# High parts of the FFN operands on GpSimd, softplus read from PSUM, x1 in two slots, new step tables, in a Mamba block with a ternary FFN

## The chip, the core and the metric

The kernel runs on one core of a Trainium2 chip. Engine names are those of the profile: PE is TensorE's matrix multiplication and PEld its weight load, DVE is VectorE, ACT is ScalarE, POOL is GpSimd, SP is SyncE. PSUM is the memory that PE writes, SBUF the working memory. The metric is the device time of one execution in microseconds (us), the median of the runs.

## The reference

Sixteen sequences of 512 tokens and 256 channels pass a selective scan layer and a feed-forward network, each followed by a residual sum and a layer norm:

```python
xr = x @ in_w.T; xx, res = split(xr)            # 512 + 512 channels
xx = silu(causal_conv4(xx) + conv_b)
delta, B, C = split(xx @ xproj_w.T)             # 16, 16, 16
delta = softplus(delta @ dt_w.T + dt_b)
h[l] = exp(delta*A) * h[l-1] + delta*B*xx       # 16 states a channel
y = (sum over states of h*C + xx*D) * silu(res)
x1 = layernorm(x + y @ out_w.T)
h = silu(x1@w1.T*w1_s) * (x1@w2.T*w2_s)         # 1024 wide
h = gelu(h@h1.T*h1_s); h = gelu(h@h2.T*h2_s)
out = layernorm(x1 + h@w3.T*w3_s)
```

The weights of the FFN hold -1, 0 and 1 times a factor. Everything is float32.

## The kernel before

A sequence is a "row". Four rows are in work at a time: `rows(i, par)` gives the one whose scan runs in iteration i (`scan` = i), the one whose inputs to the scan are made (`front` = i+1), the one whose scan is over and that is gated, projected, normed and sent into the FFN (`tail` = i-1), and the one whose FFN ends (`end` = i-2). An iteration has 64 steps, one for each of 16 states times 4 blocks of 128 channels. Every engine runs the same loop over the steps, `iteration(i, par)`, and tables of step numbers say in which step it issues which piece of the other rows' work. So the order on each engine is written out by hand. Engines meet through semaphores alone, and a step has no fixed length. FFN steps from 64 on are those of the next iteration less 64 (`ffn_step(end, s + TILES)`).

**The scan.** For a pair of steps ACT makes `dA` (L607, exp, in a ring of 8 tiles, 4 or more steps ahead) and `dB` (L616, 7 steps ahead), PE transposes dB into `scan_ps` in PSUM (L367, `b_pair`, issued one pair ahead; there are two buffers of a pair), DVE scans the pair in an even step (L782) and multiplies it by C into `hC` in the odd one (L792, two buffers), and POOL issues a DMA that adds hC to `y2` (L968, `y_pair`). hC of pair p waits until the addition of pair p-2 has landed.

**The front.** x is transposed and projected, and the convolution is made by ACT and DVE (L630, L806). PE multiplies for delta in four blocks c in the steps `F_DT` (L423) into the one bank `misc_ps`. DVE adds the bias one step later and frees the bank (L818, `dt_ready`). Softplus is max(z,0) + log(1+exp(-|z|)) with a correction of the rounding in 1+exp: Abs and Exp on ACT (L650, L652, into `du`), 1+e on DVE (L829, into `sp_w[c]`, `F_PLUS`), the lost part on DVE (L831), max less the lost part on DVE (L837, `F_MAX`), Ln on ACT (L656, step 51), the sum (L843) and times u (L848) on DVE in the steps 54 and 55.

**The FFN.** Weights are exact in float32r. Each operand is split in two float32r parts, high and low, and PE multiplies both. `half_tile` (32 of them a row, table `HALF_AT`) makes 8 matmuls of 128x512 on half of the inputs of one tile; L479 is the line of `products`, which all FFN matmuls go through. A tile of 128 outputs then goes ACT Gelu (L688, into the ring `x32` of 4 tiles), ACT Copy to the high part (L697, `hi_tiles`; in the first layer L710), POOL subtraction to the low part (L990, `low_tile`). The Gelu of tile i waits for the low part of tile i-4, and PE waits for low parts at the start of a layer. The first layer's `l1_tile` (8 of them, steps 22 to 29) is 8 matmuls, a Tanh (L705) and two DVE operations (L899, L906) of a tile. `w3_tile` (`E_W3`) makes the last product. DVE scales it (L914), adds x1 (L921) and makes the statistics (L862) and the norm (L873).

```python
dst = hb_hi if i < HC else ha_hi
nc.scalar.activation(dst[:, i % HC, :], x32[:, i % X32, :], ACT.Copy).then_inc(ffn_hi, 1)
...
pool.wait_ge(ffn_hi, f * FFN_TILES + (i + 1))
nc.gpsimd.tensor_tensor(lo[:, i % HC, :], x32[:, i % X32, :], hi[:, i % HC, :].bitcast(F32),
                        ALU.subtract).then_inc(ffn_lo, 1)
```

In the steps that hold a Gelu (`NO_EXP`) ACT makes no dA; these are made in steps before, since Exp and Gelu need different tables (ACT_TABLE_LOAD).

Of the kernel before, what the change touches and what calls it, by code (L numbers as in the profile page):

```python
# [1070 lines left out]
```

## Time and profile before

| | |
|---|---|
| median of 3 runs | 3148.1 us (3145.47 to 3153.55) |
| the profiled execution, its time and its span | 3155.7 us, 3153.9 us |
| PE, DVE, ACT, POOL busy | 2583.1, 2621.1, 2343.3, 1071.0 us |
| first scan begins, last scan ends | 83.2 us, 3001.3 us |
| the 15 rows after the first | 284.9 to 3001.3 us, 181.1 us each |
| mean granted TensorE clock | 0.897 |

The span is the time from the first to the last instruction on the core. A busy time is the union of an engine's instructions. A stretch of the trace is named here by the steps of the scan: "steps 40 to 56" is the time from the start of DVE's scan of step 40 to that of step 56. Other engines are some steps ahead or behind.

### The profile page before, as it was taken

What the parts mean: (1) busy time and instruction counts of PE and PEld (TensorE: products, weight loads), DVE (VectorE), ACT (ScalarE), POOL (GpSimd) and SP (SyncE); (2) the same over time, 40 slices, a digit from 0 to 9 for tenths busy, and PEclk for the clock granted to TensorE, in tenths of its full rate; (3) what the DMA queues carried; (4) which work ended last, traced back from release to release, by engine and by line L of the source; (5) the groups of instructions that cost most, each with busy time, mean ns of one, the idle gap of its engine ahead of it and who ended that gap; (6) DMA issues with size and microseconds to landing.
All of it is one profiled execution on the core that took longest, in us unless ns stands there. A gap on an engine that the chain in (4) does not pass through costs nothing.

```text
span 3153.9 us, 41504 instructions
## 1 busy us (share of the span) xinstructions
PE 2583.1 (82%) x12290; PEld 1944.8 (62%) x12290; DVE 2621.1 (83%) x2625; ACT 2343.3 (74%) x3653; POOL 1071.0 (34%) x1028
## 2 busy tenths in 40 slices
PE   4355788888888888988888898888888889898888
PEld 1223566676666666676666766666676756666666
DVE  3678998989898897989889898988989898998830
ACT  2776687877969787796968779697877969687822
POOL 0112333333433433343343334234333423423432
PEclk8566899999989999999989999899999989899999
DMA  1996787787878778787887878787787878778933
GB/s 52 290 321 140 167 193 180 185 197 184 194 179 193 190 181 186 183 194 183 190 188 179 194 181 194 179 196 189 178 190 181 200 186 196 189 180 191 229 111 110
DMA packets 230192, 585.49 MB, mean 186 GB/s; under 512 B 26016, under 2 KB 26400, under 8 KB 229808
## 3 DMA queue, kind: packets, MB, share of 16 engines
q0 software_dynamic: 73728, 268.47, 46.2%
q1 hardware_dynamic: 119344, 246.86, 22.4%
q10 hardware_dynamic: 36864, 67.13, 7.9%
q8 instruction: 115, 1.88, 0.2%
q14 instruction: 141, 1.16, 0.1%
HBM read 281.93 MB, written 31.98 MB: 100 GB/s over the span
## 4 chain that ended last, share of the span: by engine, by line
PE 32%; DVE 29%; ACT 17%; issue 14%; DMA 4%; ACTq 1%; DVEq 1%; SPq 1%; POOL 1%; POOLq 0%
PE ffn_ps L479 17%; DVE scan_ps L782 11%; DVE hC L792 5%; PE scan_ps L367 5%; ACT dB L616 4%; ACT dA L607 3%; DVE y L806 3%; PE misc_ps L372 3%; DMA x<-ffn_w 3%; PE misc_ps L423 2%; DVE gate L899 2%; PE misc_ps L460 2%; PE misc_ps L408 2%; ACT L607 2%; PE misc_ps L367 2%
## 5 line engine op out<-in xcount | busy, mean ns | idle before, releaser
L782 DVE TENSOR_TENSOR_SCAN scan_ps<-dA,scan_ps 128x1024 f32<-128x1024 f32 x512 | 1170.8, 2287 | 57.0 <-PE scan_ps L367 33.2
L968 POOL DMA_DIRECT2D y<-hC x512 | 446.1, 871 | 1811.2 <-DVE hC L792 1735.1
L367 PE MATMUL scan_ps<-ident,dB 128*128 128x128 f32 x4096 | 613.4, 300 | 375.7 <-DVE hC L792 292.3
L367 PEld LDWEIGHTS scan_ps<-ident,dB 128*128 128x128 f32 x4096 | 519.9, 154 | 521.2 <-DVE hC L792 305.5
L616 ACT ACTIVATE dB<-duT,bT 128x512 f32<-128x512 f32 x1024 | 726.4, 711 | 154.5 <-PE scan_ps L367 153.2
L607 ACT ACTIVATE dA<-delta,a_neg 128x512 f32<-128x512 f32 (+1 forms) x1024 | 710.1, 712 | 41.1 <-DVE hC L792 38.0
L479 PE MATMUL ffn_ps<-hb_hi,ring 128*128 128x512 f32 x1536 | 660.1, 430 | 18.4 <-DVE gate L899 8.7
L792 DVE TENSOR_TENSOR hC<-scan_ps,c_rows_sb 128x1024 f32<-128x1024 f32 x512 | 623.6, 1218 | 49.8 <-DMA y<-hC 41.5
L479 PE MATMUL ffn_ps<-hb_lo,ring 128*128 128x512 f32 x1536 | 620.7, 404 | 0.0
L479 PE MATMUL ffn_ps<-ha_hi,ring 128*128 128x512 f32 x1024 | 443.5, 433 | 2.4 <-POOL ha_lo L990 2.4
L479 PE MATMUL ffn_ps<-ha_lo,ring 128*128 128x512 f32 x1024 | 407.7, 398 | 0.0
L990 POOL TENSOR_TENSOR ha_lo<-x,ha_hi 128x512 fp32r<-128x512 f32 x256 | 356.0, 1492 | 89.8 <-ACT ha_hi L697 52.8
L479 PEld LDWEIGHTS ffn_ps<-hb_hi,ring 128*128 128x128 f32 x1536 | 304.6, 198 | 108.4 <-DVE gate L899 29.6
L479 PEld LDWEIGHTS ffn_ps<-hb_lo,ring 128*128 128x128 f32 x1536 | 303.4, 198 | 64.2 <-issue 7.4
L372 PE MATMUL misc_ps<-out_st,inw 128*128 128x512 f32 x512 | 282.3, 679 | 27.5 <-DVE y L806 25.5
L479 PEld LDWEIGHTS ffn_ps<-ha_hi,ring 128*128 128x128 f32 x1024 | 197.8, 193 | 94.9 <-issue 55.5
L479 PEld LDWEIGHTS ffn_ps<-ha_lo,ring 128*128 128x128 f32 x1024 | 197.8, 193 | 48.9 <-issue 12.8
L688 ACT ACTIVATE x<-ffn_ps,fs 128x512 f32<-128x512 f32 x256 | 166.9, 685 | 72.1 <-PE ffn_ps L479 69.7
L990 POOL TENSOR_TENSOR hb_lo<-x,hb_hi 128x512 fp32r<-128x512 f32 x128 | 194.3, 1570 | 33.2 <-ACT hb_hi L697 33.0
L705 ACT ACTIVATE gate<-ffn_ps,s_half 128x512 f32<-128x512 f32 x128 | 87.7, 685 | 116.0 <-PE ffn_ps L479 116.0
L372 PEld LDWEIGHTS misc_ps<-out_st,inw 128*128 128x128 f32 x512 | 100.6, 216 | 115.9 <-issue 74.3
L806 DVE SCALAR_TENSOR_TENSOR y<-misc_ps,conv_half,y 128x511 f32<-128x511 f32 (+2 forms) x192 | 143.3, 747 | 31.0 <-ACT y L630 26.5
(90 smaller groups left out, 2941.9 us busy)
## 6 DMA issues: line engine op xcount, KB each, us to landing
y<-hC POOLq DMA_DIRECT2D x512, 512.0 KB, 5.8
ring<-split_weights SPq DMA_DIRECT2D x704, 256.0 KB, 4.3
c_rows_sb<-c_rows ACTq DMA_DIRECT2D x256, 256.0 KB, 4.0
xt<-x_tok SPq DMA_DIRECT2D x32, 512.0 KB, 6.1
x<-ffn_w SPq DMA_DIRECT2D x22, 512.0 KB, 9.7
split_weights<-ha_hi SPq DMA_DIRECT2D x22, 512.0 KB, 5.2
split_weights<-ha_lo SPq DMA_DIRECT2D x22, 512.0 KB, 7.0
out_tok<-out_st SPq DMA_DIRECT2D x16, 512.0 KB, 2.9
```

Of the source, the lines that this page charges most:

```text
L367: mm = nc.tensor.transpose(dst[:, j * P:(j + 1) * P], src(j), ident[:])
L372: mm = nc.tensor.matmul(misc_ps[:], inw[:, k, col * P:(col + 1) * P], xT[:, k, :], start=(k == 0), stop=(k == KD - 1))
L479: mm = nc.tensor.matmul(dst, w, a, start=(first and n == 0), stop=(last and n == len(steps) - 1))
L607: nc.scalar.activation(dA[:, s % DA_RING, s % 2:], delta2[:, par, c, s % 2:], ACT.Exp, scale=a_neg[:, c, n:n + 1]).then_inc(dA_ready, 1)
L616: nc.scalar.activation(dB[:, n % 2, t, :], duT[:, t, :], ACT.Copy, scale=bT2[:, par, t, n:n + 1]).then_inc(dB_ready, 1)
L688: nc.scalar.activation(x32[:, i % X32, :], ffn_ps[(2 * HC + i) % 3][:], ACT.Gelu, scale=fs[:, 2 + i // HC, i % HC:i % HC + 1]).then_inc(ge ...
L705: nc.scalar.activation(gate[:, o % 2, :], ffn_ps[2 * o % 3][:], ACT.Tanh, scale=s1_half[:, o:o + 1]).then_inc(l1_tanh, 1)
L782: nc.vector.tensor_tensor_scan(b, dA[:, a:a + 2, :].rearrange("p a l -> p (a l)"), b, 0.0, ALU.mult, ALU.add).then_inc(scan_done, 1)
L792: nc.vector.tensor_tensor(hC[:, p % 2], scan_ps[:, h:h + 2, :], c_rows[:, n % 2].unsqueeze(1).to_broadcast([P, 2, SEQ]), ALU.mult).then_in ...
L806: nc.vector.scalar_tensor_tensor(out=y2[:, par, c, back:], in0=misc_ps[:, 0:SEQ - back], scalar=conv_half[:, c, tap:tap + 1], in1=y2[:, pa ...
L968: pool.dma_start(y2[:, par, c:c + 2, :], hC[:, p % 2], accum_op=ALU.add).then_inc(y_added[p % 2], 16)
L990: nc.gpsimd.tensor_tensor(lo[:, i % HC, :], x32[:, i % X32, :], hi[:, i % HC, :].bitcast(F32), ALU.subtract).then_inc(ffn_lo, 1)
```

## The change

1. `hi_tiles` and `low_tile` become one `split_tile` on POOL: a `tensor_copy` makes the high part, and the subtraction follows. ACT loses 24 Copy operations of 128x512 a row, and POOL gets 24 copies.
2. Delta before softplus is not stored. ACT reads the PSUM bank twice, with the bias: Abs into `du` and Relu into `delta2`, then Exp. DVE loses the addition L818 and the maximum L837. The lost part and max(z,0) are joined in another way: POOL adds exp(-|z|) to Relu(z) (`base_step`, `F_BASE`), DVE makes (w-1) less that sum (`F_LOST`), and the last operation on DVE is Ln less this (the lines L831 and L843 of before, with other operands).
3. `x1` has two slots, so that the next row may write it before the row that ends has read it.
4. The step tables are new, two PE waits are added that guard the banks of PSUM, and EXP_COUNT puts the dA tiles that a Gelu step leaves out into the latest steps before it that hold fewer than three.
5. The SBUF space for the descriptors of POOL's DMAs is set to 8192 bytes a partition.

```diff
-HALF_AT = [33, 34, 35, 36, 37, 38, 40, 41, 42, 43, 44, 45, 47, 48, 49, 50,
-           54, 55, 56, 57, 58, 59, 61, 62, 63, 64, 65, 66, 68, 69, 70, 71]
-GELU_AT = {39: (0, 1), 40: (2,), 46: (3, 4), 47: (5,), 51: (6, 7), 52: (),
-           60: (8, 9), 61: (10,), 67: (11, 12), 68: (13,), 72: (14, 15), 73: ()}
-HI_AT = {40: (0,), 41: (1,), 42: (2,), 47: (3,), 48: (4,), 49: (5,), 52: (6, 7),
-         61: (8,), 62: (9,), 63: (10,), 68: (11,), 69: (12,), 70: (13,), 73: (14, 15)}
-T_RES, T_GATE = (0, 3, 6, 8), (2, 5, 7, 10)
-T_OUT, T_ADD, T_STATS, T_NORM, T_X1T = (12, 13, 14, 15), (15, 17), (16, 18), 19, (20, 21)
-E_W3, E_SCALE, E_ADD, E_STATS, E_NORM = (11, 12, 13, 14), (15, 16), (16, 17), (19, 20), 22
-F_DT, F_EXP, F_PLUS, F_MAX, F_LN = (41, 42, 43, 44), (43, 44, 45, 48), (44, 45, 46, 49), (45, 46, 47, 50), 51
-F_DELTA, F_DELTA_U, F_Y, F_DU = (54, 54, 55, 55), (54, 54, 55, 55), (57, 58, 59, 60), (56, 57, 58, 59)
+T_RES, T_GATE = (0, 3, 5, 8), (3, 4, 7, 11)      # the tables of after, in fewer lines
+T_OUT, T_ADD, T_STATS, T_NORM = (12, 13, 15, 17), (15, 18), (16, 18), 19
+E_W3, E_SCALE, E_ADD, E_STATS, E_NORM = (10, 11, 13, 14), (12, 16), (14, 19), (15, 21), 22
+L1_AT = (22, 23, 24, 25, 26, 27, 28, 29)
+L1_SPLIT_AT = (22, 24, 25, 27, 28, 29, 30, 31)
+HALF_AT = (31, 32, 34, 35, 36, 38, 40, 41, 42, 43, 45, 46, 47, 48, 49, 50, 51, 52, 53, 54, 55, 57, 59, 60, 62,
+           63, 64, 65, 66, 68, 69, 71)
+GELU_AT = (38, 38, 39, 46, 46, 47, 50, 51, 56, 57, 58, 66, 66, 67, 72, 72)
+SPLIT_AT = (37, 40, 43, 48, 48, 49, 51, 52, 60, 60, 61, 66, 66, 67, 72, 73)
+F_XT, F_DBL, F_BT, F_BT_OUT, F_LN, T_XT = (25, 29), 39, 46, 53, 51, (62, 63)
+F_DT, F_PLUS, F_BASE, F_LOST = (40, 41, 43, 44), (46, 47, 48, 48), (42, 42, 43, 46), (47, 50, 52, 53)
+F_DELTA, F_DELTA_U, F_Y, F_DU = (53, 53, 53, 53), (53, 53, 53, 53), (53, 56, 56, 62), (54, 55, 56, 58)
...
+                if s - 1 in F_DT:                                        # ACT
+                    act.wait_ge(pe_dt, r * DC + (c + 1))
+                    nc.scalar.activation(du[:, c, :], misc_ps[:], ACT.Abs, bias=...).then_inc(sp_abs, 1)
+                    nc.scalar.activation(delta2[:, par, c, :], misc_ps[:], ACT.Relu, bias=...).then_inc(dt_ready, 1)
...
-                    nc.vector.tensor_scalar(delta2[:, par, c, :], misc_ps[:], ch[:, c, C_DTB:C_DTB + 1], None,
-                                            ALU.add).then_inc(dt_ready, 1)
...
-                    nc.vector.scalar_tensor_tensor(out=delta2[:, par, c, :], in0=delta2[:, par, c, :], scalar=0.0,
-                                                   in1=du[:, c, :], op0=ALU.max, op1=ALU.subtract).then_inc(sp_max, 1)
...
+            def base_step(r, par, s):                                    # POOL
+                    pool.wait_ge(dt_ready, r * DC + (c + 1))
+                    pool.wait_ge(sp_exp, r * DC + (c + 1))
+                    nc.gpsimd.tensor_tensor(delta2[:, par, c, :], delta2[:, par, c, :], du[:, c, :], ALU.add
+                                            ).then_inc(sp_base, 1)
...
+            def split_tile(f, i):                                        # POOL; waits for l1_x32 or gelu_x32 first
+                nc.gpsimd.tensor_copy(hi[:, i % HC, :], x32[:, i % X32, :]).then_inc(ffn_hi, 1)
+                pool.wait_ge(ffn_hi, f * FFN_TILES + (i + 1))
+                nc.gpsimd.tensor_tensor(lo[:, i % HC, :], x32[:, i % X32, :], hi[:, i % HC, :].bitcast(F32),
+                                        ALU.subtract).then_inc(ffn_lo, 1)
...
-    nc = bacc.Bacc("TRN2", target_bir_lowering=False, num_devices=1)
+    nc = bacc.Bacc("TRN2", target_bir_lowering=False, num_devices=1, dynamic_dma_scratch_size=8192)
```

## Rows read from the trace of the kernel before

**Rows 1.** Busy time by stretch: rows 1 to 15, and the end after the last scan.

```profile
core 0: us, PE busy (x) PEld busy (x) DVE busy (x) ACT busy (x) POOL busy (x), PEclk, DMA share, GB/s
284.90:3001.30 2716.40, 2326.70 (x11311) 1764.35 (x11312) 2398.84 (x2369) 2129.17 (x3318) 995.20 (x951) 0.92 0.80 188
3001.30:3153.90 152.60, 127.85 (x580) 103.77 (x578) 32.83 (x73) 39.63 (x66) 48.79 (x42) 0.92 0.32 106
```

**Rows 2.** One period: steps 56-8, 8-16, 16-24, 24-40, 40-56, and whole.

```profile
1547.90:1588.10 40.20, 38.05 (x195) 29.94 (x196) 30.85 (x24) 37.38 (x58) 15.99 (x16) 1.00 0.93 216
1588.10:1608.90 20.80, 18.73 (x113) 16.39 (x113) 15.74 (x13) 15.77 (x24) 9.79 (x9) 0.92 0.81 173
1608.90:1635.60 26.70, 19.66 (x97) 16.29 (x97) 25.64 (x44) 11.84 (x19) 5.90 (x8) 0.74 0.71 173
1635.60:1683.60 48.00, 41.30 (x179) 28.36 (x178) 45.81 (x45) 35.79 (x59) 16.34 (x16) 0.93 0.79 185
1683.60:1732.20 48.60, 41.16 (x191) 29.45 (x189) 44.35 (x42) 43.98 (x68) 19.14 (x17) 0.93 0.76 176
1547.90:1732.20 184.30, 158.90 (x768) 120.44 (x768) 162.40 (x164) 144.77 (x225) 67.16 (x64) 0.92 0.80 186
```

**Rows 3.** The chain's shares by line, first in steps 56-8, then in 40-56.

```profile
by line: PE ffn_ps L479 50.3%; PE scan_ps L367 13.6%; PE misc_ps L372 12.8%; issue 10.3%; PE misc_ps L367 5.0%; ACT dA L607 2.2%; ACT x L688 1.7%; DVE du L848 1.7%; ACT dB L616 1.6%; ACT duT L662 1.4%; ACTq L600 1.0%; ACT L688 0.2%; ACTq L6
...
by line: PE ffn_ps L479 24.8%; PE misc_ps L423 8.6%; issue 8.2%; DVE delta L843 7.1%; PE misc_ps L408 6.2%; PE scan_ps L367 5.7%; ACT dA L607 5.2%; DVE scan_ps L782 4.7%; ACT dB L616 4.1%; ACT hb_hi L697 3.4%; DVE du L848 3.2%; ACT x L688 2
```

**Rows 4.** The costliest groups: busy, mean ns of one, idle before, releaser.

```profile
L968 POOL DMA_DIRECT2D y<-hC x512 | 446.1, 871 | 1811.2 <-DVE hC L792 1735.1
L792 DVE TENSOR_TENSOR hC<-scan_ps,c_rows_sb 128x1024 f32<-128x1024 f32 x512 | 623.6, 1218 | 49.8 <-DMA y<-hC 41.5
L697 ACT ACTIVATE ha_hi<-x 128x512 fp32r<-128x512 f32 x128 | 77.5, 622 | 0.0
L837 DVE SCALAR_TENSOR_TENSOR delta<-delta,du 128x512 f32<-128x512 f32 x64 | 54.7, 857 | 0.0
L818 DVE TENSOR_SCALAR delta<-misc_ps,ch 128x512 f32<-128x512 f32 x64 | 48.0, 750 | 65.3 <-PE misc_ps L423 63.3
L862 DVE BATCH_NORM_STATS2 stats<-out_st 128x6 f32<-128x256 f32 x64 | 23.3, 406 | 0.0
L921 DVE TENSOR_TENSOR out_st<-out_st,x 128x512 f32<-128x512 f32 x32 | 21.7, 681 | 0.0
```

**Rows 5.** Duration of single instructions in ns: least, median, most.

```profile
L990 POOL TENSOR_TENSOR ha_lo<-x,ha_hi x256: 1262/1567/1620, 359.3 to 3134.9; 128x512 fp32r<-128x512 f32 x128
L980 POOL TENSOR_TENSOR var_eps<-mv,eps x32: 188/194/200, 338.4 to 3148.0; 128x4 f32<-128x4 f32 x32
L650 ACT ACTIVATE du<-delta x64: 611/614/631, 52.9 to 2805.8; 128x512 f32<-128x512 f32 x64
L630 ACT ACTIVATE y<-misc_ps,conv_half x64: 757/777/781, 19.6 to 2771.3; 128x512 f32<-128x512 f32 x64
L843 DVE TENSOR_TENSOR delta<-delta,gate x32: 673/685/1776, 66.8 to 2824.9; 128x512 f32<-128x512 f32 x32
L848 DVE TENSOR_TENSOR du<-y,delta x64: 675/680/1779, 67.4 to 2826.7; 128x512 f32<-128x512 f32 x64
```

**Rows 6.** The DMA that adds hC to y: KB each, median us from issue to landing.

```profile
y<-hC POOLq DMA_DIRECT2D x512, 512.0 KB, 5.8
```

**Rows 7.** The chain in the end stretch, in order of time: start, us, what.

```profile
3067.53 0.53 ACT ha_hi L710
...
3068.13 3.75 POOL ha_lo L990 x3
...
3101.73 0.53 ACT hb_hi L697
...
3102.33 2.50 POOL hb_lo L990 x2
...
3104.87 27.51 PE ffn_ps L479 x120
```

More of the change, by code:

```diff
@@ L61 @@
 QUARTERS = 2 * W3_SLOTS
-T_XT = (61, 62)
-T_RES, T_GATE = (0, 3, 6, 8), (2, 5, 7, 10)
-T_OUT, T_ADD, T_STATS, T_NORM, T_X1T = (12, 13, 14, 15), (15, 17), (16, 18), 19, (20, 21)
-E_W3, E_SCALE, E_ADD, E_STATS, E_NORM = (11, 12, 13, 14), (15, 16), (16, 17), (19, 20), 22
-A_L1 = 22
-A_HI, A_LO = 2, 3
-HALF_AT = [33, 34, 35, 36, 37, 38, 40, 41, 42, 43, 44, 45, 47, 48, 49, 50,
-           54, 55, 56, 57, 58, 59, 61, 62, 63, 64, 65, 66, 68, 69, 70, 71]
-GELU_AT = {39: (0, 1), 40: (2,), 46: (3, 4), 47: (5,), 51: (6, 7), 52: (),
-           60: (8, 9), 61: (10,), 67: (11, 12), 68: (13,), 72: (14, 15), 73: ()}
-HI_AT = {40: (0,), 41: (1,), 42: (2,), 47: (3,), 48: (4,), 49: (5,), 52: (6, 7),
-         61: (8,), 62: (9,), 63: (10,), 68: (11,), 69: (12,), 70: (13,), 73: (14, 15)}
-LO_AFTER = 1
-F_XT, F_XX, F_DBL, F_DBL_OUT, F_BT, F_BT_OUT = (26, 28), (30, 32, 34, 36), 39, 40, 45, 46
-F_DT, F_EXP, F_PLUS, F_MAX, F_LN = (41, 42, 43, 44), (43, 44, 45, 48), (44, 45, 46, 49), (45, 46, 47, 50), 51
-F_DELTA, F_DELTA_U, F_Y, F_DU = (54, 54, 55, 55), (54, 54, 55, 55), (57, 58, 59, 60), (56, 57, 58, 59)
+T_RES = (0, 3, 5, 8)
+T_GATE = (3, 4, 7, 11)
+T_OUT = (12, 13, 15, 17)
+T_ADD = (15, 18)
+T_STATS = (16, 18)
+T_NORM = 19
+T_X1T = (20, 21)
+E_W3 = (10, 11, 13, 14)
+E_SCALE = (12, 16)
+E_ADD = (14, 19)
+E_STATS = (15, 21)
+E_NORM = 22
+L1_AT = (22, 23, 24, 25, 26, 27, 28, 29)
[4 more added lines that the diff above has]
+SPLIT_AT = (37, 40, 43, 48, 48, 49, 51, 52, 60, 60, 61, 66, 66, 67, 72, 73)
+F_XT = (25, 29)
+F_XX = (30, 32, 34, 36)
+F_DBL = 39
+F_DBL_OUT = 40
+F_BT = 46
+F_BT_OUT = 53
+F_DT = (40, 41, 43, 44)
+F_PLUS = (46, 47, 48, 48)
+F_BASE = (42, 42, 43, 46)
+F_LOST = (47, 50, 52, 53)
+F_LN = 51
+F_DELTA = (53, 53, 53, 53)
+F_DELTA_U = (53, 53, 53, 53)
+F_Y = (53, 56, 56, 62)
+F_DU = (54, 55, 56, 58)
+T_XT = (62, 63)
 SCALE_LEAD = 7
@@ L643, in front_step @@
                                          ACT.Copy).then_inc(bT_ready, 1)
-                for c in range(DC):
-                    if F_EXP[c] != s:
-                        continue
-                    act.wait_ge(dt_ready, r * DC + (c + 1))
-                    nc.scalar.activation(du[:, c, :], delta2[:, par, c, :], ACT.Abs).then_inc(sp_abs, 1)
+                if s - 1 in F_DT:
+                    c = F_DT.index(s - 1)
+                    act.wait_ge(pe_dt, r * DC + (c + 1))
+                    nc.scalar.activation(du[:, c, :], misc_ps[:], ACT.Abs, bias=ch[:, c, C_DTB:C_DTB + 1]
+                                         ).then_inc(sp_abs, 1)
+                    nc.scalar.activation(delta2[:, par, c, :], misc_ps[:], ACT.Relu, bias=ch[:, c, C_DTB:C_DTB + 1]
+                                         ).then_inc(dt_ready, 1)
                     act.wait_ge(sp_abs, r * DC + (c + 1))
@@ L706, in ffn_step @@
                                          scale=s1_half[:, o:o + 1]).then_inc(l1_tanh, 1)
[L707 to L714 removed]
+                for i in range(2 * HC):
+                    if GELU_AT[i] == s:
+                        gelu_tile(f, i)
             def iteration(i, par):
@@ L928, in iteration @@
             def iteration(i, par):
-                (scan, _), (front, fpar), (tail, tpar), (end, _) = rows(i, par)
+                (scan, _), (front, fpar), (tail, tpar), (end, epar) = rows(i, par)
                 for s in range(TILES):
@@ L936, in iteration @@
                     if end is not None:
-                        end_step(end, s)
+                        end_step(end, epar, s)
                     if tail is not None:
@@ L1013, in iteration @@
                         ffn_step(end, s + TILES)
+                    if front is not None:
+                        base_step(front, fpar, s)
             iteration(-1, 1)
```

101 lines of the change are left out of this document (49 added, 52 removed).

## The prediction

> **What bounds the kernel now.** I read the stretches first. The 15 rows after the first take 181.1 us each (2716.4 / 15), and in them DVE is busy 88% of the time, PE 86%, ACT 78%, POOL 37% [rows 1]. So no engine alone sets the time, and a share of busy time says little here. I therefore cut one period into five stretches and ask in each which engine has no room [rows 2]:
>
> - steps 56 to 8, 40.2 us: PE 38.1, ACT 37.4, DVE 29.9. PE bounds it with ACT close behind. The chain there goes through PE matmuls for 82% (50.3 + 13.6 + 12.8 + 5.0) [rows 3].
> - steps 8 to 16, 20.8 us: PE 18.7, the others under 16.
> - steps 16 to 24, 26.7 us: DVE 25.6 (norms, statistics). DVE bounds it.
> - steps 24 to 40, 48.0 us: DVE 45.8 (first FFN layer, convolution). DVE bounds it.
> - steps 40 to 56, 48.6 us: DVE 44.4, ACT 44.0, PE 41.2. The chain is mixed; its largest piece is the FFN product [rows 3].
>
> Last, the y loop: POOL adds each hC by a DMA that lands 5.8 us after its issue [rows 6], and the multiplication two pairs on waits for the landing. One pair can't be faster than about (1.2 + 0.6 + 5.8) / 2 = 3.8 us (1.2 is the multiplication; for the gap to the issue I take 0.6 as an estimate, from a DVE operation's end to the semaphore's reader). DVE waited 41.5 us for it in all [rows 4], so it is near the bound but seldom is it.
>
> **The change, part by part, for one period.**
>
> *ACT.* 24 Copies at 0.62 us go, 14.9 us [rows 4]. Four Relus come. The trace has no Relu. Its bounds are 0.61 us (Abs from SBUF) and 0.78 us (PSUM with a bias, L630) [rows 5]; I take 0.7, +2.8 us, and +0.1 for each Abs that now reads PSUM. ACT falls by about 11.7 us, from 144.8 to 133. By stretch: 56 to 8 loses six Copies (3.7 us, to 33.7), 40 to 56 loses eight (5.0) and gains 3.2, to 42.2. New tanh steps (`T_GATE` 3) lie between Gelus, and I count no table load for them.
>
> *DVE.* L818 (4 x 0.75 = 3.0 us) and L837 (4 x 0.86 = 3.4 us) go [rows 4]; L829, L831, L843 and L848 stay in number. All 6.4 us lie in steps 40 to 56; `F_Y` 53 brings 0.5 us there. DVE goes from 44.4 to 38.5 in a stretch of 48.6, so it no longer bounds it. Two statistics (2 x 0.41) and one addition (0.68) move from steps 16 to 24 into 8 to 16 [rows 4]: 1.5 us out of a stretch that DVE bounds into one where it has 5 us of room. That is the second x1 slot's doing. Gain 1.5 us.
>
> *PE.* It loses nothing. But `HALF_AT` puts halves elsewhere: steps 56 to 71 hold 14 before and 11 after, 40 to 55 hold 12 before and 15 after. A half is 8 products. L479 in the chain is about 0.23 us a product, 1.84 us a half (from 27.5 us for 120 in the end stretch, where PE runs without a stop [rows 7]). So 5.5 us of PE move from 56 to 8 (38.1 to 32.6) into 40 to 56 (41.2 to 46.7 of 48.6).
>
> *POOL.* Each split gets a copy. No row shows a copy on POOL. Below it is bounded by the smallest operation, 0.19 us for 4 columns; above by the subtraction of two inputs, 1.57 us [rows 5]. The time beyond the fixed part goes with the inputs read, and the copy reads one of two: 0.19 + (1.57 - 0.19) / 2 = 0.88 us. I take 0.85. A split is then 2.4 us in place of 1.6. Four additions at 1.57 come. POOL rises by 24 x 0.85 + 4 x 1.57 = 26.7 us, from 67 to 94 of some 178. The sum on POOL has cover: 5 to 9 steps pass until `F_LOST` reads it, though the third stands in step 43 and waits for the Exp of ACT's step 44, with the DMA of step 45 behind it. Where the Trainium skill bears on this: its "GPSIMD Engine Reference" (section 4.1, Engine selection) says to keep elementwise work on VectorE, and calls one-input work on GpSimd roughly line-rate; the same page (3.1) has 0.77 us for 512 elements. By that the copy would be 0.08 us cheaper, and the sum would not move, since POOL bounds no stretch.
>
> *Order.* Behind a split on POOL stands the next DMA that adds to y. In steps 48 to 52 there are five splits (12 us) among three such DMAs, in 60 to 61 three, in 66 to 67 three. A DMA issued 1 to 2 us late uses up the y loop's room where steps are short. I set 1 us a period for it. On ACT, Ln at step 51 now waits for `F_LOST` of step 53: ACT may stand for two steps, some 5 us, in a stretch where it has 48.6 - 42.2 = 6.4 us idle. That covers it, just; without the cover it would cost the part over. Two guards on PE wait for work done steps before: nothing. The descriptors' space holds two DMAs in flight at most by the waits on `y_added`; no row says what it takes, and I cost it at nothing.
>
> *Sum.* 56 to 8: the larger of PE 32.6 and ACT 33.7, plus the 2.1 us by which the stretch exceeds PE now, is 36: -4.2. 8 to 16: 0. 16 to 24: -1.5. 24 to 40: 0 (the splits of the first layer: five DMAs, 4.4 us, and eight splits, 19.2 us, in 31 us). 40 to 56: between PE's 46.7 and 48.6, taken -1.5. Late DMAs: +1.0. That is -6.2 a period, -93 us for 15. Row 0 waits for the preparation of the weights: nothing.
>
> *Both ends.* In the front of row 0 the four delta products wait one after the other for their bank: Abs and Relu in place of one addition, 1.4 against 0.75 us, four times, +2.6 us. In the end stretch PE waits at layer borders for Copy and two or three subtractions (0.53, then 2.50 and 3.75 us) [rows 7]. A copy on POOL is 0.3 us longer than on ACT, and the tile in front has one too: +1.2 us at three borders. In the first layer a split (2.4, less in this quiet stretch) comes every 1.84 us, so the last is 3 to 4 us late: +7 us together. Ends: +10 us.
>
> 3155.7 - 93 + 10 = 3072.7 for the profiled execution. It lay 7.6 us above the median, so the median is 3065 us, 2.6% less.
>
> **The rivals.**
>
> *Full gain (0.21).* Freed engines also end waits between them, such as those for the gate's tanh on the full ACT. Then 40 to 56 comes down to PE's 46.7 or less, nothing is lost on late DMAs, and 2 us of waits go from 56 to 8: -6.2 - 0.4 - 1.0 - 2.0 is -9.6, 144 us: 3014 to 3040. For it: DVE idles 22 us a period [rows 2]. Against it: PE is at 97% in 40 to 56.
>
> *The y loop takes the gain (0.14).* If splits make three DMAs a period 2 us late at steps 48 to 52, 60 and 2, where the loop is tight, 6 us a period return: 3065 + 5 x 15 = 3140, and 3155 at 6. For it: POOL works in order, and a split also waits for its Gelu with DMAs behind it. Against it: DVE waited 41.5 us in 512 times so far [rows 4], with 24 subtractions a row in the same queue.
>
> *Port collisions, slower (0.12).* L843 and L848 take 0.68 us at the median and 1.78 at most [rows 5]. I read it so: a DVE operation with two SBUF inputs that meets a POOL operation waits for it, up to +1.1 us; 1 us each is taken. Elementwise time on POOL goes from some 40 to 67 us a period. Steps 40 to 56 hold some 19 DVE operations on SBUF alone (`F_PLUS`, `F_LOST`, `F_DELTA`, `F_DELTA_U`, `F_Y`). If all meet one, DVE gets 19 us more, 57.5 in place of 38.5: +10 us on 47.1, 3065 + 155 = 3220. It costs from the ninth on (47.1 - 38.5 = 8.6 us of room), and from the fifteenth on the kernel is slower than before. Against it: medians of 0.68 say that fewer than half of the operations meet one now, and eight of the 19 are in step 53, behind the last split. The same page of the Trainium skill (section 1, Specifications) has VectorE share its SBUF interfaces with GpSimd and names as contending the instructions with two SBUF inputs, as the rows show.
>
> *A dear copy (0.03).* From 1.8 us on, the eight splits of the first layer (8 x 3.4 + 4.4) fill their 31 us; at 2.5 it is +5 us there and more at borders: about 3160.
>
> *Forecast (0.50).* Own range 3040 to 3100.
>
> **Numbers.** A measurement of this kernel tells 0.3%, 9 us, from no change. Slower: most of the collisions, the dear copy and a bit of the y loop, 0.14. Same: half of the y loop, 0.07. Faster: 0.79. The range leaves out the deeper full gain and the collisions from the thirteenth on: 3015 to 3145.
>
> **What would show it.** L697 and L710 gone from ACT, ACT 11 to 12 us less a period; DVE 6 us less, all in 40 to 56; POOL some 94 us, the copy at 0.8 to 0.9 us. Steps 56 to 8 at 36 us, 16 to 24 at 25. Wrong would be: a stretch 40 to 56 over 49 us, with ACT waiting for L831's successor before Ln; hC waiting for its DMA well over 41.5 us (the y loop); medians of the two-input operations above 1 us (collisions).

## The result, and the profile after

The changed kernel takes 3025.4 us (median of 4 runs, 3022.8 to 3030.0) against 3149.4 us of before (4 runs, 3145.5 to 3153.6): ratio 0.961, 95% interval 0.959 to 0.963. That is 3.9% less. It lies inside the range (3015 to 3145), but 40 us below the value that was forecast and outside the forecast's own range (3040 to 3100), where the rival "full gain" had its times (3014 to 3040).

The page of the changed kernel, its first and second part and the two groups that are new on POOL:

```profile
span 3028.2 us, 42165 instructions
PE 2526.1 (83%) x12290; PEld 1880.9 (62%) x12290; DVE 2531.2 (84%) x2497; ACT 2185.9 (72%) x3335; POOL 1393.6 (46%) x1476
...
L793 DVE TENSOR_TENSOR_SCAN scan_ps<-dA,scan_ps 128x1024 f32<-128x1024 f32 x512 | 1171.3, 2288 | 150.1 <-PE scan_ps L387 150.0
L803 DVE TENSOR_TENSOR hC<-scan_ps,c_rows_sb 128x1024 f32<-128x1024 f32 x512 | 623.5, 1218 | 96.0 <-DMA y<-hC 89.1
L1011 POOL TENSOR_TENSOR ha_lo<-x,ha_hi 128x512 fp32r<-128x512 f32 x256 | 328.2, 1282 | 21.2
L1009 POOL CAST ha_hi<-x 128x512 fp32r<-128x512 f32 x256 | 198.0, 773 | 95.0 <-DVE x L910 66.4
```

DVE has 90 us less, ACT 157 us less, POOL 323 us more. The same stretches of the same period as in [rows 2], then the 15 rows and the end as in [rows 1]:

```profile
core 0: us, PE busy (x) PEld busy (x) DVE busy (x) ACT busy (x) POOL busy (x), PEclk, DMA share, GB/s
1494.40:1533.60 39.20, 35.29 (x182) 26.72 (x181) 30.66 (x24) 33.34 (x52) 21.25 (x23) 1.00 0.89 208
1533.60:1551.40 17.80, 16.90 (x114) 14.87 (x113) 16.58 (x14) 14.70 (x22) 10.10 (x11) 1.00 0.83 182
1551.40:1576.30 24.90, 17.70 (x94) 14.19 (x94) 24.52 (x43) 11.92 (x20) 7.94 (x11) 0.86 0.84 209
1576.30:1623.40 47.10, 39.25 (x178) 26.81 (x177) 45.69 (x46) 33.76 (x52) 21.58 (x24) 1.00 0.79 192
1623.40:1669.10 45.70, 43.43 (x209) 31.39 (x208) 39.05 (x34) 40.70 (x63) 26.33 (x26) 1.00 0.82 191
1494.40:1669.10 174.70, 152.57 (x770) 113.98 (x769) 156.49 (x155) 134.42 (x206) 87.19 (x92) 0.98 0.83 197
...
287.20:2883.90 2596.70, 2274.78 (x11325) 1705.04 (x11326) 2317.82 (x2257) 1983.60 (x3023) 1289.12 (x1362) 0.96 0.84 197
2883.90:3028.20 144.30, 123.24 (x565) 99.78 (x563) 33.45 (x73) 25.24 (x37) 66.74 (x72) 0.93 0.35 111
```

A row takes 173.1 us (2596.7 / 15), 8.0 less than the 181.1 of [rows 1]; that is 120 us. The end has 8.3 us less (144.3 for 152.6). All before the second row has 2.3 us more (287.2 for 284.9). The sum, -125.7 us, is the whole difference of the two spans.

One period is a small sample, since rows differ by a few us. So I also took the starts of the scans of rows 2 to 14 from each trace and averaged the distances. Row 15 is left out: no next row is prepared beside it, and it is shorter, which is why the period falls by 8.6 us here and the mean row by 8.0 above. This table is the main reading of the case; the rows below "after" are the experiments, told next.

```
mean us of     56 to 8  8 to 16  16 to 24  24 to 40  40 to 48  48 to 56  period
before           40.1     19.6     26.7      48.0      25.5      23.0    182.9
after            38.3     17.9     24.8      47.2      22.2      24.1    174.3
b_soft           42.0     19.7     26.7      47.8      23.7      21.1    180.9
b_hi             39.2     19.3     26.7      48.1      25.5      23.0    181.9
u_soft           38.5     17.9     24.8      47.4      25.3      26.7    180.6
u_hi             41.3     18.9     24.8      47.1      21.8      29.8    183.7
u_hi2            39.3     19.0     24.8      47.1      22.0      25.4    177.6
u_both           39.1     19.0     24.8      47.3      24.9      26.6    181.7
late_halves      42.1     18.9     24.8      47.1      21.9      24.0    178.8
u_ffn            43.7     20.8     24.8      48.1      22.9      25.1    185.4
u_tail           38.4     18.5     26.7      47.1      22.0      24.1    176.8
spread           38.5     17.8     24.8      47.2      22.3      24.1    174.7
```

### The profile page after: what moved, and what is told of

It reads as the page before. It is cut to its first block and busy times, and to the rows that moved or that the text cites. A ratio compares the mean times of both kernels' runs of the same rounds, so it can differ in the third digit from the quotient of the medians.

```text
span 3028.2 us, 42165 instructions
## 1 busy us (share of the span) xinstructions
PE 2526.1 (83%) x12290; PEld 1880.9 (62%) x12290; DVE 2531.2 (84%) x2497; ACT 2185.9 (72%) x3335; POOL 1393.6 (46%) x1476
## 5 line engine op out<-in xcount | busy, mean ns | idle before, releaser
L387 PE MATMUL scan_ps<-ident,dB 128*128 128x128 f32 x4096 | 591.3, 291 | 259.0 <-DVE hC L803 227.1
L639 ACT ACTIVATE dB<-duT,bT 128x512 f32<-128x512 f32 x1024 | 725.0, 712 | 83.2 <-PE scan_ps L387 83.1
L387 PEld LDWEIGHTS scan_ps<-ident,dB 128*128 128x128 f32 x4096 | 499.0, 149 | 410.2 <-DVE hC L803 245.8
L803 DVE TENSOR_TENSOR hC<-scan_ps,c_rows_sb 128x1024 f32<-128x1024 f32 x512 | 623.5, 1218 | 96.0 <-DMA y<-hC 89.1
L501 PE MATMUL ffn_ps<-hb_hi,ring 128*128 128x512 f32 x1536 | 655.8, 427 | 43.8 <-POOL hb_lo L1011 25.7
L501 PE MATMUL ffn_ps<-hb_lo,ring 128*128 128x512 f32 x1536 | 612.2, 399 | 0.0
L501 PE MATMUL ffn_ps<-ha_hi,ring 128*128 128x512 f32 x1024 | 436.5, 426 | 4.7 <-POOL ha_lo L1011 4.6
L501 PEld LDWEIGHTS ffn_ps<-hb_hi,ring 128*128 128x128 f32 x1536 | 297.1, 193 | 135.2 <-DVE gate L903 32.2
L1011 POOL TENSOR_TENSOR ha_lo<-x,ha_hi 128x512 fp32r<-128x512 f32 x256 | 328.2, 1282 | 21.2
L392 PE MATMUL misc_ps<-out_st,inw 128*128 128x512 f32 x512 | 260.6, 634 | 56.7 <-DVE y L817 42.8
L1009 POOL CAST ha_hi<-x 128x512 fp32r<-128x512 f32 x256 | 198.0, 773 | 95.0 <-DVE x L910 66.4
L392 PEld LDWEIGHTS misc_ps<-out_st,inw 128*128 128x128 f32 x512 | 92.6, 198 | 142.4 <-issue 65.7
L1011 POOL TENSOR_TENSOR hb_lo<-x,hb_hi 128x512 fp32r<-128x512 f32 x128 | 172.4, 1347 | 10.7
```

Of the source, the lines that this page charges most:

```text
L387: mm = nc.tensor.transpose(dst[:, j * P:(j + 1) * P], src(j), ident[:])
L392: mm = nc.tensor.matmul(misc_ps[:], inw[:, k, col * P:(col + 1) * P], xT[:, k, :], start=(k == 0), stop=(k == KD - 1))
L501: mm = nc.tensor.matmul(dst, w, a, start=(first and n == 0), stop=(last and n == len(steps) - 1))
L639: nc.scalar.activation(dB[:, n % 2, t, :], duT[:, t, :], ACT.Copy, scale=bT2[:, par, t, n:n + 1]).then_inc(dB_ready, 1)
L803: nc.vector.tensor_tensor(hC[:, p % 2], scan_ps[:, h:h + 2, :], c_rows[:, n % 2].unsqueeze(1).to_broadcast([P, 2, SEQ]), ALU.mult).then_in ...
L1009: nc.gpsimd.tensor_copy(hi[:, i % HC, :], x32[:, i % X32, :]).then_inc(ffn_hi, 1)
```

## The experiments

Each time is a median, beside runs of the kernel before on the same chip (3148.1 to 3149.7 us in the three sets); the ratio is to those. Differences to the changed kernel are to its 3025.4 us, whose own runs of before stood at 3149.4. "u_" undoes a part of the changed kernel, "b_" adds a part to the kernel before.

**u_hi: the high parts back on ScalarE.**

```diff
-                nc.gpsimd.tensor_copy(hi[:, i % HC, :], x32[:, i % X32, :]).then_inc(ffn_hi, 1)
+                nc.scalar.activation(dst[:, i % HC, :], x32[:, i % X32, :], ACT.Copy)   # in the steps of the splits
```

> The changed kernel with the high parts back on ScalarE, in the steps of the new tables (the first layer's from step 24 on, tile 0 of the second in 38), and the low parts behind them on GpSimd. Theory A (the engine without room sets each stretch, and ScalarE's relief let the stretch 56 to 8 shrink): ScalarE gets 24 x 0.62 = 14.9 us a period back, 3.7 of it in steps 56 to 8 and 5.0 in 40 to 56, where it has 4 to 5 us of room each, so 2 to 3 us a period come back: 3055 to 3070 us. Theory B (the copies on GpSimd cost through late additions to y what ScalarE's relief is worth): no change or faster, 3005 to 3030 us.

Measured: 3162.6 us, ratio 1.004 (1.003 to 1.006). Both theories missed, A by 93 us and B by 133: it is 137 us above the changed kernel. The table puts 5.7 us a period in steps 48 to 56 and 3.0 in 56 to 8. The waits of TensorE in the stretch 48 to 56 of one period, and over the whole trace of u_hi, have the cause:

```profile
PE ffn_ps L501 <- POOL hb_lo L1018: 9.0, 1, 9.0
...
PE ffn_ps L501 <- POOL hb_lo L1018: 130.9, 16, 9.0
```

TensorE stood once in each of 16 rows, up to 9.0 us, for the low part of the second layer's last tile. The timeline of ScalarE in u_hi shows what stood between that tile's Gelu (1719.78) and its high part (1727.13):

```profile
1719.78 0.68 ACT L712 ACTIVATE x<-ffn_ps,fs 128x512 f32<-128x512 f32 x1
1720.34 0.62 ACT L723 ACTIVATE hb_hi<-x 128x512 fp32r<-128x512 f32 x1
1720.99 1.28 ACT L681 ACT_TABLE_LOAD   x1
1722.28 0.63 ACT L681 ACTIVATE out_st<-out_st 128x512 f32<-128x512 f32 x1
...
1724.59 1.28 ACT L630 ACT_TABLE_LOAD   x1
1725.89 0.72 ACT L630 ACTIVATE dA<-delta,a_neg 128x512 f32<-128x512 f32 x1
1726.52 0.71 ACT L639 ACTIVATE dB<-duT,bT 128x512 f32<-128x512 f32 x1
1727.13 0.61 ACT L723 ACTIVATE hb_hi<-x 128x512 fp32r<-128x512 f32 x1
```

The Copy at 1720.34 is the tile before. My edit had put the last one a step later, behind Ln (four ACTIVATEs of L681) with a table load on either side, and behind dA and dB. So most of this result says something about my edit, not about the part.

**u_hi2: the same, with high parts of tiles 7 and 15 straight behind their Gelus.**

```diff
+HIGH_AT = (38, 40, 43, 48, 48, 49, 51, 51, 60, 60, 61, 66, 66, 67, 72, 72)   # ScalarE's steps
```

> As u_hi, high parts back on ScalarE, but each in the step of its Gelu or of the split, ahead of Ln: tile 7 in step 51 and tile 15 in step 72 straight behind their Gelus. Theory C (most of u_hi's loss is one order: the high part of tile 7 stands behind Ln, a table load and dA on ScalarE, and TensorE stood 9.0 us for its low part in one period, in the stretch 48 to 56 that was 5.7 us longer): 5 to 6 us a period come back, 3075 to 3095 us. Theory D (it is ScalarE's 14.9 us a period in general): within 20 us of u_hi's 3163 us.

Measured: 3076.5 us, ratio 0.978 (0.976 to 0.979). Theory C holds: 86 us of u_hi's 137 were that order (tile 15's copy was moved with it), and TensorE's wait for the low part fell from 130.9 to 41.4 us in all:

```profile
PE ffn_ps L502 <- POOL hb_lo L1019: 41.4, 16, 2.7
```

In the changed kernel that wait is 25.7 us, so some 16 us of what is left may still be the order. The copies' place, with that, is worth 51 us in the new tables: 1.0 us a period in 56 to 8, 1.1 in 8 to 16, 1.3 in 48 to 56.

**u_soft: the softplus of before in the new tables.**

```diff
-                    nc.scalar.activation(delta2[:, par, c, :], misc_ps[:], ACT.Relu, bias=...)
+                    nc.vector.tensor_scalar(delta2[:, par, c, :], misc_ps[:], ch[:, c, C_DTB:C_DTB + 1], None, ALU.add)
...
-                    nc.gpsimd.tensor_tensor(delta2[:, par, c, :], delta2[:, par, c, :], du[:, c, :], ALU.add)
+                    nc.vector.scalar_tensor_tensor(out=delta2, in0=delta2, scalar=0.0, in1=du, op0=ALU.max, op1=ALU.subtract)
```

> The changed kernel with the softplus of before (bias added on VectorE, maximum on VectorE, no sum on GpSimd), in the new steps. VectorE gets 6.4 us a period back in steps 40 to 56, where TensorE is busy 44 us of 46. Theory A (TensorE bounds that stretch now): at most 1 to 2 us a period, 3035 to 3055 us. Theory B (VectorE's time counts in full): 6.4 x 15 = +96 us, 3120 us.

Measured: 3114.5 us, ratio 0.989 (0.986 to 0.991). Theory B holds nearly in full (+89 of 96 us), theory A falls. The two halves of steps 40 to 56 show how; first the changed kernel, then u_soft, both of row 8:

```profile
1623.40:1645.10 21.70, 21.70 (x96) 13.66 (x95) 15.60 (x13) 18.08 (x30) 12.94 (x13) 1.00 0.81 183
1645.10:1669.10 24.00, 21.73 (x114) 17.73 (x114) 23.45 (x23) 22.62 (x34) 13.39 (x14) 1.00 0.84 198
```

```profile
1666.30:1692.60 26.30, 26.30 (x109) 16.48 (x108) 19.49 (x18) 18.45 (x29) 9.20 (x11) 0.94 0.67 157
1692.60:1719.20 26.60, 20.87 (x102) 16.79 (x101) 26.46 (x26) 23.13 (x34) 12.58 (x12) 0.87 0.72 173
...
DVE delta L828 <- PE misc_ps L444: 5.5, 3, 2.9
```

In steps 48 to 56 VectorE has no room in either kernel (23.5 of 24.0, 26.5 of 26.6), so what is put there counts in full: +2.6 us in the table. In 40 to 48 it has room (15.6 of 21.7), and yet the stretch grows by 3.1 us. VectorE stands 5.5 us before its additions for TensorE's product there, but that wait is not on top: its idle time in this half is 6.1 us in the changed kernel, at the scans, and 6.8 in u_soft. What is added is mostly the operations' own time (15.6 to 19.5 us). TensorE has no idle time in this half in either kernel; why the operations don't fit into VectorE's idle time is not shown. Some of VectorE's time is not the operations themselves: operations lengthened beside GpSimd's (told below) add 65 us in the whole trace, for 41 in the changed kernel.

**u_ffn and late_halves: the FFN's steps of before, all of them, and those of the third layer alone.**

```diff
-HALF_AT =  ... 48, 49, 50, 51, 52, 53, 54, 55, 57, 59, 60, 62, 63, 64, 65, 66, 68, 69, 71)      # late_halves
+           ... 48, 49, 50, 54, 55, 56, 57, 58, 59, 61, 62, 63, 64, 65, 66, 68, 69, 70, 71)
-GELU_AT = (..., 56, 57, 58, 66, 66, 67, 72, 72);  SPLIT_AT = (..., 60, 60, 61, 66, 66, 67, 72, 73)
+GELU_AT = (..., 60, 60, 61, 67, 67, 68, 72, 72);  SPLIT_AT = (..., 60, 61, 62, 67, 68, 69, 72, 73)
```

u_ffn has the old HALF_AT, Gelu steps and subtraction steps in all three layers; late_halves has only what is shown.

> The changed kernel with the FFN's steps of before (HALF_AT, the Gelus, and the splits in the steps of the former subtractions), all else as changed. Theory A (three halves moved out of the stretch 56 to 8, which TensorE bounds, give 4 us a period, and 5.5 us at the end where three halves fewer are left): 3025 + 60 + 5 = 3090 us. Theory B (the moved work on ScalarE and VectorE is the gain, the tables only fit it): within 15 us of 3025 us.

> The changed kernel with the halves of the third FFN layer in the steps of before (54 on, so 14 and not 11 of them in steps 56 to 71), with the Gelus and splits of these tiles moved to match; all else as changed. Theory A (TensorE bounds steps 56 to 8): three halves of 1.84 us return to that stretch, 2 to 4 us a period of them show, and the last row's FFN has three halves more to go after the last scan, +5.5 us: 3065 to 3090 us. Rival (ScalarE's relief is what shortened 56 to 8): within 15 us of 3025 us.

Measured: u_ffn 3188.0 us, ratio 1.012 (1.010 to 1.015); late_halves 3092.5 us, ratio 0.982 (0.980 to 0.983). u_ffn lost 163 us, more than either theory said. It also puts whole splits into steps where only subtractions had stood; VectorE's waits for TensorE at the scans are 218 us in all in it, for 160 in late_halves and 150 in the changed kernel. Which of its orders costs the 95 us over late_halves was not tried apart. Two more things differ in its trace: operations of VectorE lengthened beside GpSimd's add 71 us (41 in the changed kernel), and the granted clock over rows 1 to 15 is 0.92 (0.94 in late_halves, 0.96 in the changed kernel). late_halves changes less, though Gelus and splits move with the halves, and comes out 2.5 us above theory A's range (3065 to 3090): +67 us. Its stretch 56 to 8 and its stretch 40 to 56, in one period (the mean of the first is 42.1 us):

```profile
1514.90:1559.60 44.70, 41.97 (x208) 32.88 (x207) 31.00 (x24) 34.30 (x53) 21.46 (x23) 0.96 0.82 198
1650.40:1696.10 45.70, 38.62 (x178) 28.09 (x177) 39.08 (x34) 39.85 (x61) 26.31 (x26) 0.93 0.78 174
```

With three halves more (208 products and transposes for 182) TensorE is busy 42.0 of 44.7 us in 56 to 8. ScalarE has about as little to do there as in the changed kernel (34.3 and 33.3 us) and has 10 us of room: its relief doesn't shorten a stretch that TensorE fills. By itself, in the old tables, it gives 0.9 us there (b_hi). What comes back, 3.8 us, is more than the 1.8 by which the change had shortened the stretch: with 14 halves in it, it is longer now (42.1) than before (40.1), as in b_soft, told below. And steps 40 to 56 are only 0.4 us shorter in the table for having some 30 instructions of TensorE less (178 for 209 in this period). So three halves cost next to nothing where they stand now.

**u_tail: the steps of before of the gate, the projection, the norms and the last product.**

```diff
-T_RES = (0, 3, 5, 8); T_ADD = (15, 18); T_GATE = (3, 4, 7, 11); T_OUT = (12, 13, 15, 17); E_W3 = (10, 11, 13, 14); E_SCALE = (12, 16); E_ADD = (14, 19); E_STATS = (15, 21)
+T_RES = (0, 3, 6, 8); T_ADD = (15, 17); T_GATE = (2, 5, 7, 10); T_OUT = (12, 13, 14, 15); E_W3 = (11, 12, 13, 14); E_SCALE = (15, 16); E_ADD = (16, 17); E_STATS = (19, 20)
```

> The changed kernel with the tail's and the end's steps of before (gate, output projection, both norms, last product), all else as changed. By the prediction 1.5 us a period come from them, 3048 us. The traces had 3.6 us a period less in steps 8 to 24: if all of that is from these tables, 3079 us; if it is from other parts, 3030 us or less.

Measured: 3068.4 us, ratio 0.975 (0.972 to 0.977), +43 us, between the two sums of the expectation. 1.9 us a period of it stand in steps 16 to 24 and 0.6 in 8 to 16. The first is what the prediction had as 1.5; the other 1.1 us of the 1.7 that steps 8 to 16 lost are not from these tables.

**b_hi and b_soft: one part alone in the kernel before.** The diffs are those of u_hi and u_soft the other way, with the tables of before; the sum on GpSimd stands in the steps of `F_EXP` and the lost part in those of `F_MAX`.

> The kernel before with the high parts on GpSimd alone, in the steps of its subtractions; softplus, tables and x1 as before. ScalarE loses 14.9 us a period, GpSimd gains 24 copies of 0.78 us. Theory A (each stretch by the engine without room; steps 56 to 8 had TensorE at 38.1 of 40.2 beside ScalarE): 0 to 2 us a period less, 3120 to 3150 us. Theory E (ScalarE's relief is worth by itself what u_hi lost without it): 3100 us or less.

> The kernel before with the new softplus alone (both readings of PSUM on ScalarE, the sum on GpSimd in the steps of F_EXP, the lost part in those of F_MAX). VectorE loses 6.4 us a period in steps 40 to 56. Theory F (the operations count on VectorE in full wherever the tables stand, as u_soft's 89 us say): 3055 to 3075 us. Theory A (TensorE at 25.5 of 25.5 us in steps 40 to 48 keeps that half; only what lies in 48 to 56 counts, one maximum of 0.86 us and one reading): 3125 to 3150 us.

Measured: b_hi 3135.6 us, ratio 0.996 (0.994 to 0.997), inside theory A; b_soft 3122.9 us, ratio 0.992 (0.991 to 0.994), 2 us below theory A. Theories E and F fall. Alone, the parts give 12.5 and 25 us; in the new tables taking them out costs 51 and 89. b_soft shows where a gain goes. Its stretches 56 to 8 and 40 to 56 in one period:

```profile
1528.90:1571.50 42.60, 40.32 (x210) 31.82 (x209) 31.16 (x24) 39.54 (x63) 15.97 (x16) 1.00 0.88 206
...
1666.30:1711.10 44.80, 38.66 (x175) 27.76 (x174) 38.55 (x33) 43.70 (x69) 23.59 (x21) 0.90 0.83 189
```

Steps 40 to 56 got 3.7 us shorter (48.5 to 44.8 in the table), and VectorE is at 38.6, as forecast. But steps 56 to 8 got 1.9 us longer (40.1 to 42.0): TensorE was busy 38.1 of 40.2 us there before [rows 2], with the old 14 halves, and now has to make in it what it no longer has time for ahead of it (210 instructions for 195). VectorE's waits for TensorE at the scans rise from 33.2 to 142.7 us in all. Half of the gain is given back.

**u_both: the tables and the second slot alone.** u_hi2 and u_soft together.

> The changed kernel with both sets of operations as before (high parts on ScalarE in u_hi2's steps, softplus of before) in the new tables: the tables and the second x1 slot alone. u_hi2 lost 51 us and u_soft 89 us against 3025. If the losses add: 3165 us, so that the tables alone make the kernel slower than before. If the two share a cause (VectorE then bounds 40 to 56 and ScalarE's load hides behind it): 3120 to 3140 us.

Measured: 3133.0 us, ratio 0.993 (0.991 to 0.996). The second case holds in its number: the losses don't add (108 us for 51 + 89). Its cause doesn't: in steps 48 to 56 it is ScalarE that has no room (26.5 of 26.6 us), and VectorE has 2 us:

```profile
1698.70:1725.30 26.60, 21.74 (x106) 17.76 (x105) 24.56 (x27) 26.45 (x40) 9.32 (x8) 0.87 0.75 178
```

The tables alone are worth 16 us. So of 124 us the operations alone, in the old tables, give 12.5 and 25, the tables alone 16, and the rest, some 70 us, comes only from having them together (124 - 53.5). Two of the pairs can be read from the runs: the tables with the new softplus give 72 us (u_hi2 against before), 30 more than their parts, and the tables with the copies on GpSimd 35 (u_soft), 6 more. Both operations in the old tables were not run together.

**one_slot_16k: one slot for x1, and the descriptors' space as before.**

```diff
-        x1 = sb("x1", [P, 2, TT, DIM])
+        x1 = sb("x1", [P, TT, DIM])
...
+                    wait_past(dve, z2_ready, r * 2)
                     normalise(0, xt, x1, r, x1_ready)
```

> The changed kernel with one slot for x1, VectorE waiting for z2_ready before it writes x1 (the addition that reads x1 stands just ahead on the same engine), and the descriptors' space at its former size. The prediction gave the second slot the move of the end's addition and statistics. Theory H (the order on VectorE does it, the slot and the space nothing): within 9 us of 3025 us. Theory I (the wait or the space costs 1 us a period or more): 3040 us or more, or, if the small space cost, 3010 us or less.

Measured: 3026.2 us, ratio 0.960 (0.958 to 0.963). Theory H holds: slot and space together are worth nothing in time.

**base_late and spread: GpSimd's queue.** The sums in later steps, and the splits of step 60 drawn apart.

```diff
-F_BASE = (42, 42, 43, 46)                 # base_late
+F_BASE = (44, 44, 46, 47)
-SPLIT_AT = (..., 60, 60, 61, 66, 66, 67, 72, 73)     # spread
+SPLIT_AT = (..., 58, 60, 62, 66, 66, 67, 72, 73)
```

> The changed kernel with GpSimd's four sums in steps 44, 44, 46, 47 in place of 42, 42, 43, 46. GpSimd stood 169 us in all before these sums for ScalarE's Exp, and the additions to y behind them, at steps 42 and 44, were issued 3.5 and 2.4 us after hC. Theory A (TensorE sets steps 40 to 48, and VectorE waits for it there anyway): within 9 us of 3025 us. Theory G (the late additions cost): 1 us a period less, 3010 us.

> The changed kernel with the three splits of steps 60, 60, 61 in 58, 60, 62. There GpSimd issued the addition to y of step 60 1.7 us after hC, and hC of steps 58 to 62 started 0.1 us after the landing it waits for. Theory J (the y loop sets this stretch, so a later issue costs directly): 0.5 to 1 us a period less, 3010 to 3018 us. Theory A (TensorE sets 56 to 8 as a whole): within 5 us of 3025 us.

Measured: base_late 3030.2 us, ratio 0.962 (0.960 to 0.964); spread 3034.5 us, ratio 0.963 (0.961 to 0.965). GpSimd's idle time before its sums, first in the changed kernel, then in base_late, fell by 109 us:

```profile
  ACT du L677: 169.1, 63
```

```profile
  ACT du L677: 60.0, 4
```

and nothing was gained: theory A holds, theory G falls. In spread the addition to y of step 60 is issued 0.65 us after hC in place of 1.7 (median over rows 3 to 14), and the kernel is no faster, rather 9 us slower. Theory J falls as worded, and theory A's "within 5 us" is missed as well; what the 9 us are is open. But the run doesn't clear the y loop. In the changed kernel hC of each of the steps 58, 60, 62, 0 and 2 starts 0.11 or 0.12 us behind the landing it waits for (median over rows 3 to 14; before, 0.11 in step 62 alone and 0.27 in step 0). Each waits for the pair before the last, so these are two chains: 58, 62, 2 and 60, 0, 4. spread sped up the second (step 0 now starts 0.42 us behind the landing), while the first, whose additions were issued 0.6 us after hC all along and land 6.5 and 7.8 us later, stayed as it was, and so did the stretch (38.3 and 38.5 us).

## Why the prediction came out as it did

- **ACT.** Foreseen -11.7 us a period, measured 144.8 to 134.4, -10.4. Relu from PSUM 0.68 us (0.7 taken), Abs from PSUM 0.69. The tanh steps brought no table loads: 89 and 90 before Gelu and dA in the whole program, 88 and 89 in the kernel before.
- **DVE.** -6.4 us and +0.5 foreseen, 162.4 to 156.5 measured. The collisions were held apart in the forecast and did not grow: by means less the undisturbed 0.68 and 0.42 us they cost about 40 us in all after (L841 22, L835 14, others 5) and 40 before (L837 11, L843 17, L848 12). Most medians stayed; the one that moved is that of L835's gate form (L829 before), 0.42 to 0.62:

```profile
L841 DVE SCALAR_TENSOR_TENSOR delta<-out_st,delta x32: 677/684/1751, 55.7 to 2703.2; 128x512 f32<-128x512 f32 x32
L835 DVE TENSOR_SCALAR gate<-du x32: 416/622/823, 55.4 to 2691.3; 128x512 f32<-128x512 f32 x32
L852 DVE TENSOR_TENSOR du<-y,delta x64: 676/679/687, 68.3 to 2708.7; 128x512 f32<-128x512 f32 x64
```

  The four products by u in step 53 never meet a split (most 687 ns), as the rival's "against" had it, while the operations of steps 46 to 52 do. That the meeting is what costs can be read from the records: of the 46 operations of L835 during which GpSimd computed, 42 were over 15% longer than undisturbed, and none of the 18 others; for L841 it is 28 of 43 and none of 21. The Trainium skill's "GPSIMD Engine Reference" (section 1, Specifications) also names VectorE's two-port mode as contending. The trace agrees in so far as L835, with one SBUF input and 0.42 us alone, takes up to 0.82 us (row above) beside splits; that it runs in that mode no row says.
- **POOL.** Foreseen +26.7 us a period, measured +20.0 (67.2 to 87.2). Both prices were too high. A copy takes 0.61 us and a subtraction or sum 1.28 of the engine's time: 24 x 0.61 + 4 x 1.28 = 19.8. The prediction's 1.57 was the length of a record that overlaps the one before it by 0.3 us (last section), and so is the copy's mean record of 0.77 to 0.79 us. A split is 1.9 us in place of 2.4. The Trainium skill's "GPSIMD Engine Reference" (section 3.1, Elementwise — side-by-side cycle accounting) gives 0.77 us as the best case of a tight loop over 512 elements; the undisturbed copy of this trace is faster, 0.61 us, and the measurement decides.
- **16 to 24.** Foreseen -1.5, measured -1.9. The mechanism held (u_tail). The credit did not: the second slot of x1 is not needed for it (one_slot_16k).
- **56 to 8.** Foreseen -4.2 and +1.0 for late additions, -3.2; measured -1.8, and -1.7 in 8 to 16, where 0 was foreseen: -3.5 for both. TensorE was to fall by 5.5 us, to 32.6; it fell by 2.8 (38.1 to 35.3), with 13 instructions fewer and not 24. And the stretch exceeds it by 3.9 us, not 2.1. That the three halves shorten it holds: late_halves puts back 3.8 us and 1.0 in 8 to 16. What holds the stretch at 38.3 is not shown; the y loop is tight in it (see spread).
- **40 to 56: the step that failed.** Foreseen -1.5, with the sentence that VectorE "no longer bounds it"; measured -2.2, and VectorE has no room in half of it. I took 16 steps as one and compared 38.5 with 48.6. Cut in two, the stretch is 3.3 us shorter in 40 to 48 and 1.1 longer in 48 to 56. In the second half VectorE has 23.5 of 24.0 us, and 22.9 of 23.0 before. The first half of the period before was:

```profile
1683.60:1709.20 25.60, 25.60 (x115) 16.74 (x114) 21.45 (x23) 22.46 (x36) 7.40 (x7) 1.00 0.76 176
```

  There TensorE has no idle time, before and after, but 96 instructions for 115. VectorE's work fell from 21.5 to 15.6 us and its idle time rose, from 4.1 to 6.1: the waits for TensorE's product went, and waits at the scans came (33.2 to 150.0 us in the whole trace). The sum had such a shift at nothing.
- **24 to 40.** Foreseen 0, measured -0.8, which goes with the steps of the FFN: u_ffn is at 48.1 again. GpSimd was not too slow for the first layer, as the rival "a dear copy" needed.
- **The ends: the term with the wrong sign.** Foreseen +10, measured -6: front and row 0 +2.3, the end -8.3 in place of +7. The +2.3 is near the 2.6 foreseen but does not confirm it, since the first scan begins at 83.3 us for 83.2 before, and the 2.6 was to come ahead of it. The end has two causes. Fewer halves are left after the last scan: two and not the three that leave 56 to 8 (520 FFN products for 536), 3.7 us at 0.23 us each, which I did not carry to the end; late_halves has 534 and an end of 147.5 us. And the copies on GpSimd shorten it where I had them lengthen it: b_hi alone, with all 536 products, has 148.2 us for 152.6. Other kernels with the changed end have 141.5 to 144.3 us, so neither part is known to better than some 3 us. At the last border TensorE resumes 2.86 us after the Gelu's start in place of 3.83 (3132.40 to 3136.23 before), because one split stands behind it, where two subtractions had. The chain of the changed kernel there:

```profile
3010.27 0.70 ACT x L712
...
3011.13 0.62 POOL ha_hi L1009
...
3011.82 1.27 POOL ha_lo L1011
...
3013.13 6.50 PE ffn_ps L501 x52
```

  The 52 matmuls behind it took 8.0 us before, at a granted clock of 0.79, and 6.5 us now, at 1.00 (b_hi: 6.5 and 1.00 too):

```profile
3136.23:3144.26 8.03, 7.99 (x52) 7.78 (x52) 0.69 (x2) 0.00 (x0) 0.00 (x0) 0.79 0.00 0
3013.13:3019.64 6.51, 6.49 (x52) 6.29 (x52) 2.14 (x4) 0.00 (x0) 0.00 (x0) 1.00 0.00 0
```

- **The rivals.** *Full gain* gave the right time, but not by its terms: steps 40 to 56 did come to 46.3 us, below the 46.7 named, and the gate waits fell (127.9 to 37.0 us), but steps 56 to 8 gave 1.8 us and not 6.2, and the end gave what was not in it. *The y loop*: the sign that the prediction named for it did come, the landing waits of hC rose from 41.5 to 89.1 us. It did not take the gain; base_late and spread could give nothing back, and whether the loop holds steps 58 to 2 is open. *Port collisions* exist and stayed at their old sum in the changed kernel. The range was said to leave them out "from the thirteenth on"; by the prediction's own working thirteen give 3131 us, inside the range, and fourteen 3146.

In numbers, for the profiled executions: 15 x 1.8 us a period and 16 us at the ends, 43 us, lie between the 3072.7 that was forecast and the 3030.0 measured. The medians lie 40 us apart, since the profiled execution was 7.6 us above its median before and 4.6 after. That the sum by stretch came as near as it did is in part luck: 56 to 8 gave less than foreseen, and 8 to 16, 24 to 40 and the end gave what was not in it.

## What to carry to other kernels

Where every engine is 80 to 90% busy, cut a period finely enough that each piece has one engine without room (8 steps in 40 to 56, not 16), and follow what is moved out of a piece to wherever it goes on, the end of the program among it, by counting it there. Removing work and re-laying the order are worth little apart (12.5, 25 and 16 us here) and much together (124): in the traces of b_soft and late_halves a shorter stretch hands its time to the next one, which has then to be emptied too. When undoing a part to measure it, look at who stands behind the part put back: 86 of the 137 us of the first try were the place of two Copies, one of them behind Ln.
